# SyncE's order in the attention stage of a four-layer graph network: the turned pair's store and loads side by side

## The chip, the cores and the metric

The kernel runs on one core of a Trainium2 chip. The metric is the device time of one execution in microseconds (us), the median over the runs.

## The reference, cut to what matters

Four graph layers run in sequence on x of 4096 x 128 with one adjacency matrix of 4096 x 4096, each with a residual and a layer norm. The change lies in the third, a transformer convolution with four heads of width 32.

```python
x = _layernorm(x + _L0_gnn_ref(x, adj, ...), axis=-1)   # adj @ x, then a GRU cell
x = _layernorm(x + _L1_gnn_ref(x, adj, ...), axis=-1)   # normalised adj @ (x @ W)
x = _layernorm(x + _L2_gnn_ref(x, adj, ...), axis=-1)   # the attention below
x = _layernorm(x + _L3_gnn_ref(x, adj, ...), axis=-1)   # hyperbolic layer, adj @ xt

attn = jnp.einsum('nhc,mhc->hnm', q, k) / np.float32(np.sqrt(C))
mask = adj == 0.0
neg = jnp.where(mask[None], -jnp.inf, attn)
...
out = jnp.einsum('hnm,mhc->hnc', alpha, v)
```

## The kernel before

**Stages.** Layers 0 and 1 and the last one multiply the whole adjacency matrix, in 8 chunks of 512 columns that pass through a ring of 1 MB slots (`adj_cols`). Between them lies the attention, from about 570 to 1600 us of the span.

**The attention's tiles.** It works through 8 chunks of 512 rows; a chunk has 4 row blocks of 128 rows, and a row block is done in 2 sets of 2048 columns each. So there are 64 sets (set 0 to 63, eight to a chunk). A set is 16 units of 128 columns; every unit has the four heads. Everything is unrolled, and each engine has an order written out by hand, in places k (one per unit, 128 to a chunk).

- PE (TensorE): `scores` (L635, matmuls L647) writes the scores of a block of 1024 columns for one head, 13 heads ahead of the units. `turn_unit` (L667, L674) turns the probabilities of a unit into PSUM; ACT (L920) or VectorE (L1226) copies them to SBUF. `attend` (L678, L696) multiplies them with the values, four units at a time, 7 to 10 places later.
- VectorE: `mask` (L1197, L1211) adds scores and mask bias and takes the minimum. It also turns units 14 and 15 of every set itself, in 32 x 32 blocks, in `turn_blocks` (L1228, L1236) at places 3 and 5 of the next set.
- GpSimd: `mask_bias` (L1470, L1476) makes a mask bias from a loaded piece of the adjacency matrix (128 x 1024). It also runs the long row chain of the chunk before (`post_steps`, L1483 to L1489), in fixed slots between the masks.
- SyncE issues the loads and stores of the stage, in the order of `attention_loads` (L433).

**The turned pair.** Blocks that VectorE turned still lie in the wrong order of 32-row blocks. The pair (units 14 and 15 of a set, `GROUPS = ((14, 15),)`) therefore goes to DRAM in one store of 512 KB (`store_group`, L411, issue L417) and comes back in four loads of 128 KB (`load_group`, L419, issue L429). The loads wait for the store (`group_out`) and for PE to have used units 0 to 7 of the same set, whose slots they take (`unit_used`, L427). PE waits for them (`group_landed`) before unit 14, at place 19 counted from the set's first unit.

**What else is in SyncE's order.** `load_mask` (L395, issue L399) waits until GpSimd has made the bias two masks before (`bias_ready`), since the two input buffers alternate; it runs 7 masks ahead. `load_queries` (L402, issue L407) loads the queries of the row block after the next one, four DMAs of 64 KB, in every odd set. `store_xt` (L458, L460), in sets 48 and 56, saves a result tile `mx_g` that GpSimd overwrites in the next chain; `store_x3` (L480, L482) does the same for x3 once per chunk; `load_residuals` (L468, L477) ends the chunk. An instruction of SyncE that waits holds everything behind it in the order.

For each set the order is: the first mask; then in the second half the store, the second mask, `store_xt`, queries, `store_x3`, and last the pair's four loads.

Of the kernel before, what the change touches and what calls it, by code (L numbers as in the profile page):

```python
# [117 lines left out]

def groups_until(g):

    return g // UPS * len(GROUPS) + sum(group[-1] < g % UPS for group in GROUPS)


def block_turns(g):
# [4 lines left out]
def group_of(k):  # L129

    return [group for group in GROUPS if k % UPS in group][0]


def in_group(k):

    return group_of(k).index(k % UPS)

# [46 lines left out]
def build_program(nc, adj_cols, adj, x_tiles, x_t, w_msg, b_msg, w_ih, w_hh, b_ih, b_hh, w_gcn, b_gcn,  # L184
# [7 lines left out]
    xt_dram = nc.dram_tensor("xt_dram", [len(SPILLED), P, CHUNK], F32)  # L192
    group_dram = nc.dram_tensor("group_dram", [2, P, 2 * CHUNK], F32)
    k4_dram = nc.dram_tensor("k4_dram", [CHUNKS, 4, H, C, CHUNK], F32)

    with ExitStack() as ctx:
# [70 lines left out]
        group_slots = arena[:, RING + 10 * CHUNK:RING + 12 * CHUNK]  # L267
        group_blocks = stat_s[:, TILES - 2 * TPC:TILES, :].rearrange("p t f -> p (t f)")
        spilled = stat_s[:, SPILLED[0] * TPC:(SPILLED[-1] + 1) * TPC, :].rearrange("p t f -> p (t f)")
        adj_in = (arena[:, RING + 4 * CHUNK:RING + 6 * CHUNK], spilled)  # L270
        maskbias = [half_[:, i * BLOCK:(i + 1) * BLOCK] for half_ in
# [9 lines left out]

        def slots_of(group):
            i = group[0] % TURNED - 6
            return group_slots[:, i * CHUNK:(i + len(group)) * CHUNK]

# [40 lines left out]
        bias_ready = sem("bias_ready")  # L326
        xt_out, xt_in_place = sem("xt_out"), sem("xt_in_place")
        scores_ready = sem("scores_ready")
# [5 lines left out]
        unit_used = sem("unit_used")  # L334
        blocks_turned = sem("blocks_turned")
        group_out = sem("group_out")
        group_landed = sem("group_landed")
        rows_pe, rows_act, rows_dve, rows_pool = [sem(f"rows_{e}") for e in ("pe", "act", "dve", "pool")]
# [28 lines left out]
        def _(sp):  # L367
            def load_ring(layer, c, first, slots=SLOTS):

                for s in range(slots):  # L370
                    turn = layer * CHUNKS + c
                    if layer == 0 and first:
                        sp.dma_start(stat_x[:, s * JPS:(s + 1) * JPS, :].rearrange("p t f -> p (t f)"),
                                     x_tiles[:, s * JPS * P:(s + 1) * JPS * P]).then_inc(x_in[s], 16)
                    if first and layer == 2 and s % 4 == 0:
                        turned_before = (CHUNKS * SPC - 2 + s // 4 + 1) * UPS
                        sp.wait_ge(unit_turned, pe_turns(turned_before))
                        sp.wait_ge(blocks_turned, block_turns(turned_before))
                    if not first:
                        sp.wait_ge(ring_multiplied, (turn - 1) * SLOTS + s + 1)  # L380
                        if layer == 0 or is_zero(c):
                            sp.wait_ge(ring_summed, (turn - 1) * SLOTS + s + 1)
                    sp.dma_start(ring[:, s, :, :].rearrange("p j i -> p (j i)"),
                                 adj_cols[bass.ds(c, 1), s, :, :].rearrange("c p n -> (c p) n")
                                 ).then_inc(ring_landed[s], 16)
# [24 lines left out]

            def store_group(g):  # L411

                i, n = groups_until(g), len(group_of(g))
                sp.wait_ge(blocks_turned, block_turns(g + n))
                if i >= 2:
                    sp.wait_ge(group_landed, 16 * (P // C) * (i - 1))
                sp.dma_start(group_dram[i % 2, :, 0:n * CHUNK], group_blocks[:, 0:n * CHUNK]).then_inc(group_out, 16)  # L417

            def load_group(g):  # L419

                i, n = groups_until(g), len(group_of(g))
                slots = slots_of(group_of(g))
                sp.wait_ge(group_out, 16 * (i + 1))
                if i < len(GROUPS):
                    sp.wait_ge(gcn_x2_out, 16 * CHUNKS)
                if g + n > TURNED:
                    sp.wait_ge(unit_used, g + n - TURNED)  # L427
                for j in range(P // C):
                    sp.dma_start(slots[j * C:(j + 1) * C, :].rearrange("k (q n) -> k q n", q=P // C),  # L429
                                 group_dram[i % 2, :, j * n * P:(j + 1) * n * P].rearrange("(q k) n -> k q n", q=P // C)  # L430
                                 ).then_inc(group_landed, 16)

            def attention_loads(c):  # L433
                for st in range(SPC):
                    for half_set in range(2):
                        groups = [group for group in GROUPS if group[0] // UPB == half_set]
                        ahead = c * COLS + 2 * st + half_set + MASK_AHEAD
                        if half_set == 1:
                            for group in groups:
                                store_group(c * UPC + st * UPS + group[0])  # L440
                        if ahead < CHUNKS * COLS:
                            load_mask(ahead // COLS, ahead % COLS, False)
                        if half_set == 0:
                            for group in groups:
                                store_group(c * UPC + st * UPS + group[0])
                        if half_set == 1 and st == 0 and c - 2 in SPILLED:
                            store_xt(c - 2)
                        if half_set == 1 and st % SETS == 1:
                            ahead = c * TPC + st // SETS + 2
                            if ahead < CHUNKS * TPC:  # L450
                                load_queries(ahead // TPC, ahead % TPC, False)
                        if half_set == 1 and st == 4 and c > 0:
                            store_x3(c - 1)
                        for group in groups:
                            load_group(c * UPC + st * UPS + group[0])
                load_residuals(c)
# [5 lines left out]
            def load_xt():  # L462
                sp.wait_ge(bias_ready, CHUNKS * COLS)
                for i in range(len(SPILLED)):
                    sp.wait_ge(xt_out, 16 * (i + 1))
                    sp.dma_start(spilled[:, i * CHUNK:(i + 1) * CHUNK], xt_dram[i, :, :]).then_inc(xt_in_place, 16)
# [57 lines left out]
        def _(pe):  # L524
# [153 lines left out]
            def attend(c, k, first):  # L678
# [4 lines left out]
                if is_block_turned(k):  # L683
                    pe.wait_ge(group_landed, 16 * (P // C) * (groups_until(c * UPC + k) + 1))
                elif k in BY_VECTOR:
                    pe.wait_ge(unit_copied_dve, c * len(BY_VECTOR) + BY_VECTOR.index(k) + 1)
                else:
                    pe.wait_ge(unit_copied_act, c * len(BY_SCALAR) + BY_SCALAR.index(k) + 1)
                for h in range(H):
                    to = bank[h * C:(h + 1) * C, 7, st * P:(st + 1) * P]  # L690
                    if is_block_turned(k):
                        to = to.rearrange("c (q r) -> c q r", q=P // C)
                        weights = group_tiles(slots_of(group_of(k)), len(group_of(k)))[:, in_group(k), h, :, :]
                    else:
# [332 lines left out]
        def _(dve):  # L1027
# [169 lines left out]
            def mask(c, m, h, first):  # L1197
# [3 lines left out]
                if h == 0:  # L1201
                    dve.wait_ge(bias_ready, c * COLS + m + 1)
                    if not (first and m < 4):
                        dve.wait_ge(unit_turned, pe_turns((c * COLS + m - 3) * UPB))
                        dve.wait_ge(blocks_turned, block_turns((c * COLS + m - 3) * UPB))
                if hi:
# [21 lines left out]
            def turn_blocks(c, k):  # L1228

                st, u = k // UPS, k % UPS  # L1230
                i = groups_until(c * UPC + k)
                dve.wait_ge(exp_ready, (c * SPC + st) * H + H)
                if i > 0:
                    dve.wait_ge(group_out, 16 * i)
                n = len(group_of(k))
                dve.transpose(group_tiles(group_blocks[:, 0:n * CHUNK], n)[:, in_group(k), :, :, :],  # L1236
                              cols[:, st % SETS, :, u * P:(u + 1) * P].rearrange("p h (j k) -> p h j k", j=P // C)
                              ).then_inc(blocks_turned, 1)

# [162 lines left out]
        def _(pool):  # L1402
# [76 lines left out]
            def post_steps(c, factor_at=31):  # L1479
# [96 lines left out]
                def factor():  # L1576
# [3 lines left out]
                    tt("fac", s1, s1, t1, ALU.mult)  # L1580
                    if isinstance(c, int) and c == CHUNKS - 2:
                        pool.wait_ge(group_out, 16 * CHUNKS * SPC * len(GROUPS))
                    to = tiles(mx_g) if c in SPILLED else stat_s[:, c * TPC:(c + 1) * TPC, :]
# [112 lines left out]
```

## Time and profile before

| | |
|---|---|
| median of 3 runs | 1848.42 us (1846.78 to 1848.55) |
| the profiled execution | 1854.71 us |
| its span, first to last instruction | 1852.9 us |
| busy share PE / VectorE / ScalarE / GpSimd | 95% / 67% / 52% / 48% |
| mean granted TensorE clock over the span | 0.978 |

A row of a wait names the instruction that waited, then what ended the wait. In a timeline a line gives the start, the length, engine, source line and operation, and in brackets the idle time before it. `SPq` is SyncE's queue, whose instructions are issues and take about 0.3 to 0.45 us each; "x4" merges four. The granted clock is TensorE's, 1.00 for 2.4 GHz.

### The profile page before, as it was taken

To read this page: it belongs to the slowest core of one execution; us is meant where nothing else is said; L and a number is where in the kernel's file an instruction comes from. 1 tells how busy PE (TensorE), PEld (TensorE's weight loads), DVE (VectorE), ACT (ScalarE), POOL (GpSimd) and SP (SyncE) were. 2 spreads that over 40 slices of the span, in tenths; PEclk is the share of its full clock that TensorE was granted. 3 is DMA by queue.
4 is the path that set the end of the run, shared out by engine and by line. 5 is a ranking of instruction groups with operands and counts; after the bars stand their busy time and mean duration, and the time that the engine had idled before them with its cause. 6 is when DMAs were issued, how large, how long until landed. Compare 5 with 4: busy or idle time off the path is not lost.

```text
span 1852.9 us, 40409 instructions
## 1 busy us (share of the span) xinstructions
PE 1764.6 (95%) x14992; PEld 1163.3 (63%) x14992; DVE 1249.3 (67%) x2454; ACT 959.6 (52%) x1456; POOL 897.4 (48%) x853
## 2 busy tenths in 40 slices
PE   7999999999996999999999999999999999799996
PEld 3444444444444888877878878878778787444442
DVE  4777775222216999998989989979989899201322
ACT  0110110100004989898989978978989899201101
POOL 0111110111126556778687687777786886340111
PEclk9999999999997999999999999999999999899998
DMA  9857666799987555445444555454454543797791
GB/s 374 306 215 264 248 235 240 273 376 379 393 299 244 154 160 162 146 136 162 148 148 144 155 155 149 138 149 143 139 166 148 150 153 105 281 373 283 276 333 65
DMA packets 138525, 396.92 MB, mean 214 GB/s; under 512 B 16240, under 2 KB 67184, under 8 KB 113776
## 3 DMA queue, kind: packets, MB, share of 16 engines
q1 hardware_dynamic: 115776, 353.42, 55.9%
q10 hardware_dynamic: 20016, 32.78, 4.9%
q0 software_dynamic: 2560, 8.39, 1.5%
q8 instruction: 111, 1.82, 0.4%
q14 instruction: 62, 0.51, 0.1%
HBM read 333.19 MB, written 61.34 MB: 213 GB/s over the span
## 4 chain that ended last, share of the span: by engine, by line
PE 73%; POOL 10%; DMA 6%; DVE 4%; issue 3%; SPq 2%; ACT 0%; POOLq 0%; ACTq 0%; DVEq 0%
PE bank L540 32%; PE bank L674 14%; PE bank L647 10%; PE bank L696 9%; POOL arena L1476 3%; POOL small L1483 3%; DMA arena<-group_dram 2%; POOL early L1476 2%; DVE arena L1211 2%; DMA arena<-adj_cols 2%; DMA q_dram<-arena 1%; PE bank L528 1%; SPq L429 1%; PE bank L561 1%; PE bank L562 1%
## 5 line engine op out<-in xcount | busy, mean ns | idle before, releaser
L908 ACT ACTIVATE arena<-arena,small 128x2048 f32<-128x2048 f32 x256 | 512.3, 2001 | 0.0
L674 PE MATMUL bank<-ident,arena 128*128 128x128 f32 x3584 | 477.6, 275 | 0.7 <-ACT arena L908 0.7
L674 PEld LDWEIGHTS bank<-ident,arena 128*128 128x128 f32 x3584 | 423.4, 142 | 66.5 <-issue 3.5
L540 PE MATMUL bank<-arena,stat_s 128*128 128x512 f32 x1008 | 444.7, 598 | 9.7 <-DMA arena<-adj_cols 6.3
L920 ACT ACTIVATE arena<-bank 128x512 f32<-128x512 f32 x624 | 351.1, 596 | 112.4 <-PE bank L674 109.3
L647 PE MATMUL bank<-k,parts 128*128 128x512 f32 x1024 | 375.6, 449 | 13.3 <-DVE small L1211 7.1
L540 PEld LDWEIGHTS bank<-arena,stat_s 128*128 128x128 f32 x1008 | 191.2, 192 | 238.4 <-issue 236.7
L696 PE MATMUL bank<-arena,stat_x 128*32 128x128 f32 x8192 | 280.9, 277 | 27.2 <-DMA arena<-group_dram 27.2
L696 PEld LDWEIGHTS bank<-arena,stat_x 128*32 128x32 f32 x8192 | 207.9, 110 | 85.9 <-issue 48.8
L540 PE MATMUL bank<-arena,stat_x 128*128 128x512 f32 x512 | 230.8, 602 | 10.8 <-DMA arena<-adj_cols 8.5
L1226 DVE COPY arena<-bank 128x512 f32<-128x512 f32 x272 | 181.9, 676 | 44.0 <-PE bank L674 43.9
L647 PEld LDWEIGHTS bank<-k,parts 128*128 128x128 f32 x1024 | 157.3, 193 | 70.8 <-issue 41.6
L1211 DVE CUSTOM_DVE_ANT_0 arena<-bank,early,small 128x1024 f32<-128x1024 f32 x128 | 160.2, 1274 | 24.6 <-issue 18.5
L540 PEld LDWEIGHTS bank<-arena,stat_x 128*128 128x128 f32 x512 | 96.4, 192 | 127.4 <-issue 127.0
L1211 DVE CUSTOM_DVE_ANT_0 arena<-bank,arena 128x1024 f32<-128x1024 f32 x128 | 155.2, 1218 | 12.9 <-PE bank L674 8.9
L1211 DVE CUSTOM_DVE_ANT_0 arena<-bank,arena,small 128x1024 f32<-128x1024 f32 x128 | 160.5, 1278 | 1.5 <-PE bank L647 0.5
L1211 DVE CUSTOM_DVE_ANT_0 arena<-bank,early 128x1024 f32<-128x1024 f32 x128 | 155.2, 1213 | 6.7 <-PE bank L647 4.1
L1422 POOL TENSOR_SCALAR small<-small 128x4 f32<-128x4 f32 x32 | 13.0, 407 | 262.0 <-DVE small L1038 262.0
L1476 POOL TENSOR_SCALAR early<-arena 128x1024 bf16<-128x1024 f32 x32 | 116.3, 3634 | 32.2 <-DVE small L1211 25.6
L1476 POOL TENSOR_SCALAR arena<-arena 128x1024 bf16<-128x1024 f32 x32 | 116.5, 3641 | 24.2 <-DVE small L1211 13.9
L1476 POOL TENSOR_SCALAR early<-stat_s 128x1024 bf16<-128x1024 f32 x32 | 116.1, 3628 | 22.7 <-DVE small L1211 19.1
L1476 POOL TENSOR_SCALAR arena<-stat_s 128x1024 bf16<-128x1024 f32 x32 | 116.8, 3649 | 10.5 <-DVE small L1211 4.4
(155 smaller groups left out, 1425.7 us busy)
## 6 DMA issues: line engine op xcount, KB each, us to landing
arena<-adj_cols SPq DMA_DIRECT2D x190, 1024.0 KB, 6.4
arena<-adj SPq DMA_DIRECT2D x64, 512.0 KB, 4.8
stat_s<-adj SPq DMA_DIRECT2D x64, 512.0 KB, 4.4
group_dram<-stat_s SPq DMA_DIRECT2D x64, 512.0 KB, 3.0
arena<-group_dram SPq DMA_DIRECT2D x256, 128.0 KB, 2.9
k_dram<-arena ACTq DMA_DIRECT2D x32, 256.0 KB, 6.9
q_dram<-arena ACTq DMA_DIRECT2D x32, 256.0 KB, 11.7
k<-k_dram POOLq DMA_DIRECT2D x32, 256.0 KB, 8.4
```

The source lines that it names most:

```text
L429: sp.dma_start(slots[j * C:(j + 1) * C, :].rearrange("k (q n) -> k q n", q=P // C), group_dram[i % 2, :, j * n * P:(j + 1) * n * P].rearra ...
L528: last = pe.transpose(bank[:, dst_bank, t * P:(t + 1) * P], src[:, t * P:(t + 1) * P], ident[:, :])
L540: mm_ = pe.matmul(bank[:, to, :], stat[:, jt, :], ring[:, s, j, :], start=(jt == 0), stop=(jt == TILES - 1))
L647: last = pe.matmul(bank[:, u + i, :], parts[:, t % 2, h * P:(h + 1) * P], k4[:, h, at_:at_ + CHUNK], start=True, stop=True)
L674: last = pe.transpose(bank[:, b_, h * P:(h + 1) * P], cols[:, st % SETS, h, u * P:(u + 1) * P], ident[:, :])
L696: last = pe.matmul(to, stat_x[:, k % UPT, h * C:(h + 1) * C], weights, start=(u == 0), stop=(u == UPS - 1))
L908: act.activation(cols[:, s_, h, :], cols[:, s_, h, :], ACT.Exp, bias=shift[:, t % 2, 1, i:i + 1], scale=-1.0, accum_out=blocksum[:, t % 2, ...
L920: act.activation(turned[k % TURNED], bank[:, TURN_BANKS.bank(("unit", k)), :], ACT.Copy).then_inc(unit_copied_act, 1)
L1211: dve.tensor_tensor_reduce(out=cols[:, s_, h, hi * BLOCK:(hi + 1) * BLOCK], in0=bank[:, 2 * (h % 2):2 * (h % 2) + 2, :].rearrange("p b n - ...
L1226: dve.tensor_copy(turned[k % TURNED], bank[:, TURN_BANKS.bank(("unit", k)), :]).then_inc(unit_copied_dve, 1)
L1476: pool.tensor_scalar(maskbias[m % 4], adj_in[m % 2], 0.0, MASKED, ALU.is_equal, ALU.mult).then_inc(bias_ready, 1)
L1483: step(c, name, pool.tensor_tensor(out_, a, b, op))
```

## The change

In each set SyncE now issues: the first mask, the pair's store, the pair's four loads, the second mask, `store_xt`, queries, `store_x3`. The waits inside `load_group` stay, so SyncE stands there until the store has landed and PE has freed the slots.

The semaphores `blocks_turned`, `group_out` and `group_landed` become lists with one entry per group, and are counted in sets. There is still one group. The DRAM buffer has one place per group instead of two in turn, so a store waits for the landing of the loads of the set before, not of two sets before. VectorE's `mask` no longer waits for its own `blocks_turned`; the reloading of the spilled tiles (`load_xt`) waits for all stores as well.

```diff
-    group_dram = nc.dram_tensor("group_dram", [2, P, 2 * CHUNK], F32)
+    group_dram = nc.dram_tensor("group_dram", [len(GROUPS), P, 2 * CHUNK], F32)
...
-        group_blocks = stat_s[:, TILES - 2 * TPC:TILES, :].rearrange("p t f -> p (t f)")
         spilled = stat_s[:, SPILLED[0] * TPC:(SPILLED[-1] + 1) * TPC, :].rearrange("p t f -> p (t f)")
-        adj_in = (arena[:, RING + 4 * CHUNK:RING + 6 * CHUNK], spilled)
+        adj_in = (arena[:, RING + 4 * CHUNK:RING + 6 * CHUNK], spilled[:, 0:2 * CHUNK])
+        tail = stat_s[:, TILES - 2 * TPC:TILES, :].rearrange("p t f -> p (t f)")
+        blocks = [tail if len(group) == 2 else spilled[:, 2 * CHUNK:3 * CHUNK] for group in GROUPS]
...
-            def store_group(g):
-
-                i, n = groups_until(g), len(group_of(g))
-                sp.wait_ge(blocks_turned, block_turns(g + n))
-                if i >= 2:
-                    sp.wait_ge(group_landed, 16 * (P // C) * (i - 1))
-                sp.dma_start(group_dram[i % 2, :, 0:n * CHUNK], group_blocks[:, 0:n * CHUNK]).then_inc(group_out, 16)
-
-            def load_group(g):
-
-                i, n = groups_until(g), len(group_of(g))
-                slots = slots_of(group_of(g))
-                sp.wait_ge(group_out, 16 * (i + 1))
-                if i < len(GROUPS):
+            def store_group(g, i):
+
+                n = len(GROUPS[i])
+                sp.wait_ge(blocks_turned[i], n * (g + 1))
+                if g > 0:
+                    sp.wait_ge(group_landed[i], 16 * (P // C) * g)
+                sp.dma_start(group_dram[i, :, 0:n * CHUNK], blocks[i]).then_inc(group_out[i], 16)
+
+            def load_group(g, i):
+
+                n, slots = len(GROUPS[i]), slots_of(i)
+                sp.wait_ge(group_out[i], 16 * (g + 1))
+                if g == 0:
                     sp.wait_ge(gcn_x2_out, 16 * CHUNKS)
-                if g + n > TURNED:
-                    sp.wait_ge(unit_used, g + n - TURNED)
+                if g * UPS + GROUPS[i][-1] >= TURNED:
+                    sp.wait_ge(unit_used, g * UPS + GROUPS[i][-1] - TURNED + 1)
                 for j in range(P // C):
                     sp.dma_start(slots[j * C:(j + 1) * C, :].rearrange("k (q n) -> k q n", q=P // C),
-                                 group_dram[i % 2, :, j * n * P:(j + 1) * n * P].rearrange("(q k) n -> k q n", q=P // C)
-                                 ).then_inc(group_landed, 16)
+                                 group_dram[i, :, j * n * P:(j + 1) * n * P].rearrange("(q k) n -> k q n", q=P // C)
+                                 ).then_inc(group_landed[i], 16)
+
+            def load_mask_ahead(c, n):
+                ahead = c * COLS + n + MASK_AHEAD
+                if ahead < CHUNKS * COLS:
+                    load_mask(ahead // COLS, ahead % COLS, False)
 
             def attention_loads(c):
                 for st in range(SPC):
-                    for half_set in range(2):
-                        groups = [group for group in GROUPS if group[0] // UPB == half_set]
-                        ahead = c * COLS + 2 * st + half_set + MASK_AHEAD
-                        if half_set == 1:
-                            for group in groups:
-                                store_group(c * UPC + st * UPS + group[0])
-                        if ahead < CHUNKS * COLS:
-                            load_mask(ahead // COLS, ahead % COLS, False)
-                        if half_set == 0:
-                            for group in groups:
-                                store_group(c * UPC + st * UPS + group[0])
-                        if half_set == 1 and st == 0 and c - 2 in SPILLED:
-                            store_xt(c - 2)
-                        if half_set == 1 and st % SETS == 1:
-                            ahead = c * TPC + st // SETS + 2
-                            if ahead < CHUNKS * TPC:
-                                load_queries(ahead // TPC, ahead % TPC, False)
-                        if half_set == 1 and st == 4 and c > 0:
-                            store_x3(c - 1)
-                        for group in groups:
-                            load_group(c * UPC + st * UPS + group[0])
+                    g = c * SPC + st
+                    load_mask_ahead(c, 2 * st + 0)
+                    store_group(g, 0)
+                    load_group(g, 0)
+                    load_mask_ahead(c, 2 * st + 1)
+                    if st == 0 and c - 2 in SPILLED:
+                        store_xt(c - 2)
+                    if st % SETS == 1:
+                        ahead = c * TPC + st // SETS + 2
+                        if ahead < CHUNKS * TPC:
+                            load_queries(ahead // TPC, ahead % TPC, False)
+                    if st == 4 and c > 0:
+                        store_x3(c - 1)
                 load_residuals(c)
...
                 sp.wait_ge(bias_ready, CHUNKS * COLS)
+                for i in range(len(GROUPS)):
+                    sp.wait_ge(group_out[i], 16 * CHUNKS * SPC)
...
                 if is_block_turned(k):
-                    pe.wait_ge(group_landed, 16 * (P // C) * (groups_until(c * UPC + k) + 1))
+                    i = group_of(k)
+                    pe.wait_ge(group_landed[i], 16 * (P // C) * ((c * UPC + k) // UPS + 1))
...
-                        dve.wait_ge(blocks_turned, block_turns((c * COLS + m - 3) * UPB))
...
-                i = groups_until(c * UPC + k)
+                i = group_of(k)
                 dve.wait_ge(exp_ready, (c * SPC + st) * H + H)
-                if i > 0:
-                    dve.wait_ge(group_out, 16 * i)
-                n = len(group_of(k))
-                dve.transpose(group_tiles(group_blocks[:, 0:n * CHUNK], n)[:, in_group(k), :, :, :],
+                if c * SPC + st > 0:
+                    dve.wait_ge(group_out[i], 16 * (c * SPC + st))
```

## Rows read from the trace of the kernel before

**Rows 1.** The page's first part: busy time of each engine over the span.

```profile
PE 1764.6 (95%) x14992; PEld 1163.3 (63%) x14992; DVE 1249.3 (67%) x2454; ACT 959.6 (52%) x1456; POOL 897.4 (48%) x853
```

**Rows 2.** Waits of PE, 595 to 1600 us: total us, times, longest us.

```profile
PE bank L696 <- DMA arena<-group_dram: 27.2, 13, 3.5
PE bank L528 <- DVE arena L1047: 5.3, 7, 0.8
```

**Rows 3.** Timeline of PE in two stretches: start us, us, then the group.

```profile
842.56 0.65 PE L696 MATMUL bank<-arena,stat_x 128*32 128x128 f32 x16 [2.97 <-DMA arena<-group_dram]
...
1595.48 1.08 PE L696 MATMUL bank<-arena,stat_x 128*32 128x128 f32 x16 [3.35 <-DMA arena<-group_dram]
```

**Rows 4.** Waits of SyncE's own queue, whole span: total us, times, longest us.

```profile
SPq L427 <- PE bank L696: 152.3, 52, 6.3
```

**Rows 5.** Timeline of SyncE's queue, 811 to 837 us (sets 14 and 15).

```profile
811.87 0.34 SPq L417 DMA_DIRECT2D group_dram<-stat_s  x1
818.31 0.33 SPq L399 DMA_DIRECT2D arena<-adj  x1
818.74 3.11 SPq L429 DMA_DIRECT2D arena<-group_dram  x4
...
828.95 0.34 SPq L417 DMA_DIRECT2D group_dram<-stat_s  x1
834.07 0.33 SPq L399 DMA_DIRECT2D arena<-adj  x1
834.44 1.85 SPq L407 DMA_DIRECT2D parts<-q_dram  x4
836.39 1.80 SPq L429 DMA_DIRECT2D arena<-group_dram  x4
```

**Rows 6.** Windows around two PE waits: us, PE busy (matmuls), granted clock, DMA share, GB/s.

```profile
840.00:850.00 10.00, 7.44 (x78) 0.83 0.69 211
...
1220.00:1230.00 10.00, 6.50 (x52) 0.66 0.56 167
```

**Rows 7.** Timeline of SyncE's queue in an ordinary odd set (set 9).

```profile
735.41 0.34 SPq L417 DMA_DIRECT2D group_dram<-stat_s  x1
735.79 0.43 SPq L399 DMA_DIRECT2D arena<-adj  x1
736.26 2.26 SPq L407 DMA_DIRECT2D parts<-q_dram  x4
740.54 1.74 SPq L429 DMA_DIRECT2D arena<-group_dram  x4
```

**Rows 8.** Timeline of PE in the same set: the first scores of the next row block.

```profile
748.62 0.71 PE L647 MATMUL bank<-k,parts 128*128 128x512 f32 x2
```

**Rows 9.** DMA issues by tile: KB each, median us from issue to landing.

```profile
arena<-adj SPq DMA_DIRECT2D x64, 512.0 KB, 4.8
parts<-q_dram SPq DMA_DIRECT2D x128, 64.0 KB, 3.8
```

**Rows 10.** Source line L407, the query loads: spread of the landing times.

```profile
DMA to landing us min/median/max: 1.9/3.8/5.5
```

**Rows 11.** Timelines of GpSimd and VectorE: the mask of set 9's second half.

```profile
744.06 3.63 POOL L1476 TENSOR_SCALAR early<-arena 128x1024 bf16<-128x1024 f32 x1
...
766.14 1.21 DVE L1211 CUSTOM_DVE_ANT_0 arena<-bank,early 128x1024 f32<-128x1024 f32 x1
```

**Rows 12.** Timelines of SyncE, GpSimd and VectorE, set 48 and after: the spilled tile.

```profile
1357.51 0.79 SPq L460 DMA_DIRECT2D xt_dram<-arena  x1
1362.81 2.45 SPq L429 DMA_DIRECT2D arena<-group_dram  x4
...
1364.76 1.28 POOL L1483 TENSOR_TENSOR arena<-arena,wbr 128x512 f32<-128x512 f32 x1
...
1385.96 1.29 POOL L1483 TENSOR_TENSOR arena<-arena 128x512 f32<-128x512 f32 x1
...
1390.40 0.87 DVE L1031 BATCH_NORM_STATS2 small<-arena 128x6 f32<-128x128 f32 x4
```

More of the change, by code:

```diff
@@ L116, in pe_turns @@
     return g // UPC * len(PE_UNITS) + sum(k < g % UPC for k in PE_UNITS)
-def groups_until(g):
-    return g // UPS * len(GROUPS) + sum(group[-1] < g % UPS for group in GROUPS)
 def block_turns(g):
@@ L129, in group_of @@
 def group_of(k):
-    return [group for group in GROUPS if k % UPS in group][0]
+    return [i for i, group in enumerate(GROUPS) if k % UPS in group][0]
 def in_group(k):
-    return group_of(k).index(k % UPS)
+    return GROUPS[group_of(k)].index(k % UPS)
 class TurnBanks:
@@ L280, in group_tiles, with slots_of @@
             return ap.rearrange("p (b u h n) -> p u h b n", b=P // C, u=n, h=H)
-        def slots_of(group):
-            i = group[0] % TURNED - 6
-            return group_slots[:, i * CHUNK:(i + len(group)) * CHUNK]
+        def slots_of(i):
+            first, n = GROUPS[i][0] % TURNED - 6, len(GROUPS[i])
+            return group_slots[:, first * CHUNK:(first + n) * CHUNK]
         def tiles(ap):
@@ L326, in build_program @@
         bias_ready = sem("bias_ready")
-        xt_out, xt_in_place = sem("xt_out"), sem("xt_in_place")
         scores_ready = sem("scores_ready")
@@ L334, in build_program @@
         unit_used = sem("unit_used")
-        blocks_turned = sem("blocks_turned")
-        group_out = sem("group_out")
-        group_landed = sem("group_landed")
+        blocks_turned = [sem(f"blocks_turned{i}") for i in range(len(GROUPS))]
+        group_out = [sem(f"group_out{i}") for i in range(len(GROUPS))]
+        group_landed = [sem(f"group_landed{i}") for i in range(len(GROUPS))]
+        xt_out, xt_in_place = sem("xt_out"), sem("xt_in_place")
         rows_pe, rows_act, rows_dve, rows_pool = [sem(f"rows_{e}") for e in ("pe", "act", "dve", "pool")]
@@ L375, in load_ring @@
                     if first and layer == 2 and s % 4 == 0:
-                        turned_before = (CHUNKS * SPC - 2 + s // 4 + 1) * UPS
-                        sp.wait_ge(unit_turned, pe_turns(turned_before))
-                        sp.wait_ge(blocks_turned, block_turns(turned_before))
+                        sets = CHUNKS * SPC - 2 + s // 4 + 1
+                        sp.wait_ge(unit_turned, pe_turns(sets * UPS))
+                        for i, group in enumerate(GROUPS):
+                            sp.wait_ge(blocks_turned[i], sets * len(group))
                     if not first:
@@ L692, in attend @@
                         to = to.rearrange("c (q r) -> c q r", q=P // C)
-                        weights = group_tiles(slots_of(group_of(k)), len(group_of(k)))[:, in_group(k), h, :, :]
+                        weights = group_tiles(slots_of(i), len(GROUPS[i]))[:, in_group(k), h, :, :]
                     else:
@@ L1230, in turn_blocks @@
                 st, u = k // UPS, k % UPS
-                i = groups_until(c * UPC + k)
+                i = group_of(k)
                 dve.wait_ge(exp_ready, (c * SPC + st) * H + H)
-                if i > 0:
-                    dve.wait_ge(group_out, 16 * i)
-                n = len(group_of(k))
-                dve.transpose(group_tiles(group_blocks[:, 0:n * CHUNK], n)[:, in_group(k), :, :, :],
+                if c * SPC + st > 0:
+                    dve.wait_ge(group_out[i], 16 * (c * SPC + st))
+                dve.transpose(group_tiles(blocks[i], len(GROUPS[i]))[:, in_group(k), :, :, :],
                               cols[:, st % SETS, :, u * P:(u + 1) * P].rearrange("p h (j k) -> p h j k", j=P // C)
-                              ).then_inc(blocks_turned, 1)
+                              ).then_inc(blocks_turned[i], 1)
             def below_max(c, t):
@@ L1580, in factor @@
                     tt("fac", s1, s1, t1, ALU.mult)
-                    if isinstance(c, int) and c == CHUNKS - 2:
-                        pool.wait_ge(group_out, 16 * CHUNKS * SPC * len(GROUPS))
+                    if c == CHUNKS - 2:
+                        for i in range(len(GROUPS)):
+                            pool.wait_ge(group_out[i], 16 * CHUNKS * SPC)
                     to = tiles(mx_g) if c in SPILLED else stat_s[:, c * TPC:(c + 1) * TPC, :]
```

## The prediction

> **What bounds the kernel now.** I began with the busy times [rows 1]: PE, TensorE's matmuls, is busy 95% of the span and no other engine over 67%. The reader is to see that a microsecond counts only if PE loses it. The second view, PE's waits in the attention stage, lists little: 27.2 us in 13 waits for `arena<-group_dram`, and 5.3 us in seven small ones for VectorE [rows 2]. PE runs its 64 sets there almost without a gap, so the loads of the turned pair are what can be won.
>
> The timeline of PE gives the places [rows 3]. The thirteenth wait, 3.35 us at 1595.48, closes the last set, where no mask or query load is left and PE has no other work; the change doesn't touch what it waits for. The other twelve sum to 27.2 - 3.35 = 23.8 us, and lie in the last two sets of each of chunks 1 to 6.
>
> SyncE's queue says why [rows 4, 5]. Of 64 pair loads, 52 start when PE frees the slots (L427); twelve start later. In set 14 the store goes out at 811.87, the next instruction is a mask load that waits for GpSimd until 818.31, and the pair's loads follow it at 818.74. In set 15 the store is at 828.95, the mask at 834.07, four query loads take 1.85 us, and the pair starts at 836.39. Here GpSimd is behind with the row chain of the chunk before, and its mask delays loads that have nothing to do with masks.
>
> The granted clock adds to the price [rows 6]. PE's windows show 0.83 after the 2.97 us wait at 842.56 and 0.66 after the longest. Four windows of 10 us show 0.83 (1.7 us lost at most in each, since in part of it the clock is at 1.2 instead of 2.4 GHz) and one 0.66 (3.4 us): 10.2 us together.
>
> **The change, part by part.** *The pair's store and loads are put together, ahead of the set's second mask.* The twelve late loads then start at the later of the store's landing and PE's release. PE's release comes, as in an ordinary set, some 5.1 us after the store (735.41 to 740.54 [rows 7]): in set 14 at about 817.0 instead of 818.74, in set 15 at about 834 or earlier instead of 836.39. This removes 23.8 us of waits and, if the clock then stays up, up to 10.2 us. I take 10 of these, with 0 and 10.2 as bounds. In the second of each two sets the store itself can land late, beside the set's first mask; I keep 1 us in all for six such sets (bounds 0 and 6, up to 1 us each).
>
> *Mask loads go later.* In an ordinary set the second mask was issued 0.4 us after the store, at 735.79; now it follows the pair's loads, at 740.54 + 1.74 = 742.3, some 6.5 us later [rows 7]. It lands 4.8 us later [rows 9], at 747.1, and GpSimd, which started on it at 744.06, is delayed by 3 us; but VectorE reads the result first at 766.14 [rows 11]: 18 us of cover. In the sets where GpSimd is late its own backlog sets the mask's time, and nothing changes. Cost 0; without that cover it would be up to 3 us a set.
>
> *Query loads go later, and here the cover is thin.* In every odd set, 30 times, four query loads used to start at 736.26; now they come after the pair and the mask. From the start of the pair's loads L: 1.74 us for these, 0.43 and a gap for the mask, three more issues of 0.47, so the last query DMA starts at L + 3.7 and lands 3.8 us later by the median [rows 9]: L + 7.5, and L + 7.7 where the bytes queue a little. PE reads them for the first scores of the next row block at 748.62, L + 8.1 [rows 8]. The margin was over 6 us; it becomes some 0.4 us. Landing times run from 1.9 to 5.5 us [rows 10], and four pair loads take 3.11 us instead of 1.74 in some sets [rows 5], so about half of these sets would come late, by some 0.5 to 1.5 us. What is queued behind: PE's scores, then everything. I put the mean over all 30 at 0.4 us, 12 us in sum (estimate). Bounds: 0 if all lands in time; with every query 1 us later than by these medians, mean about 0.9, 27 us.
>
> By the Trainium skill (DMA: Bandwidth & Descriptors, Anatomy of one DMA) a DMA takes about 2.0 us fixed plus its bytes over 436 GB/s, a fit of the GpSimd path. For 64 KB that is 2.15 us, the last query DMA would land at about L + 5.9, no set would wait, and the sum would be 31 us of gain instead of 19. The trace has 3.8 us here, and I go by the trace.
>
> *Stores of `xt` and `x3` go later.* In sets 48 and 56 the spilled tile's store moves from 1357.51 to behind the pair and the mask, about 1365, and lands near 1370 instead of 1362; GpSimd overwrites the tile at 1364.76, so it waits some 5 us. Its row chain ends at 1385.96 + 1.29 and VectorE reads it at 1390.40: 3.2 us of cover [rows 12]. Two times 2 us are left on VectorE, half of which I let reach PE: 2 us (bounds 0 and 4). The `x3` store has half a chunk of time; cost 0.
>
> *Semaphores per group, one DRAM buffer instead of two, a VectorE wait dropped.* There is one group, so the counts name the same events. The store now waits for the previous set's loads, which PE has multiplied with before that store is due. VectorE's dropped wait was for its own long finished work. At 0, bounds -1 and +1.
>
> Sum: 23.8 + 10 - 1 - 12 - 2 = 19 us (18.8). The profiled execution took 1854.7 us (span 1852.9), so it would be 1836; the median of the runs, 1848.4, is 6.3 below it, and 1848.4 - 18.8 gives 1829.5.
>
> **The rivals.** *A. The likeliest: the waits go, late queries take a third back.* 1829.5, own range 1821 to 1839.
>
> *B. The queries are in time.* For it: by the medians they land 0.4 us early. 33.8 - 3 leaves 30.8 us of gain: 1817.6. Against: the spread in rows 10 and the slow issues in rows 5.
>
> *C. The queries come over 1 us late in most odd sets.* The pair's four loads move 512 KB in small pieces, the mask another 512 KB, and the queries stand behind both. 30 waits of 0.9 us give back 27 of the 30.8 and leave 1844.6. It decides against the change from about 1.2 us over the medians, where 30 waits of 1.03 us equal the 30.8 won; at 1.5 us over (30 waits of 1.3) the kernel takes 1848.4 - 30.8 + 39 = 1856.6. For it: the landing spread in rows 10. Against: before the change the queries stood behind a store and a mask of the same size. The Trainium skill (same page, Queues, rings and completion order) says that each DMA engine takes the descriptors of one issuing engine's queue in ring order; by that rule the queries are served last, which is this case.
>
> *D. It doesn't do what it says.* If the late loads were held by L427 or by the store's landing, PE's waits would remain: within 3 us of before. Rows 5 speak against it, since both had come before 818.31 and 834.07.
>
> **How the numbers follow.** A 0.55, B 0.2, C 0.22, D 0.03. A change under 0.2%, 3.7 us, is about what a measurement of this kernel can't tell from none. Of C, 0.12 end faster, 0.04 within that bound and 0.06 slower. Faster: 0.55 + 0.2 + 0.12 = 0.87; same: 0.04 + 0.03 of D = 0.07; slower: 0.06. Range: from 1815, the full 33.8 us, to 1844, the cheap end of C.
>
> **What would show it.** Right: PE's waits for `arena<-group_dram` fall to about 3.4 us in one or two, and the granted clock is 1.00 from 600 to 1590. SyncE's queue shows the pair's loads about 5 us after the store in every set. A new row, PE L647 waiting for `parts<-q_dram`, sums to about 12 us in 10 to 20 waits. GpSimd waits once or twice some 5 us in chunks 6 and 7 before its L1483. Wrong: if that new row stays under 3 us (B), or passes 25 us or pulls the clock down (C), or if the old row stays (D).

## The result, and the profile after

The changed kernel takes 1843.05 us (median of 13 runs, 1836.95 to 1848.52), the kernel before 1848.56 us (13 runs, 1846.3 to 1855.68). The ratio is 0.9965, 95% interval 0.9952 to 0.9979: faster, by 5.5 us between the medians, 3.9 to 8.9 us by the interval. The forecast was 1829.5, a gain of 18.8 us. The measured time lies inside the range of 1815 to 1844 us, but outside case A's own range of 1821 to 1839. The traced executions took 1854.71 us before and 1848.52 us after, the slowest of the changed kernel's 13, so their figures run above those of a median execution.

The waits of PE in the attention stage, 595 to 1600 us, come first again (total us, times, longest us). They answer to [rows 2].

```profile
PE bank L642 <- DMA parts<-q_dram: 15.4, 16, 3.0
PE bank L523 <- DVE arena L1043: 5.3, 7, 0.8
PE bank L535 <- DMA arena<-adj_cols: 5.2, 1, 5.2
PE bank L642 <- DVE small L1206: 4.2, 7, 1.7
PE bank L692 <- DMA arena<-group_dram: 3.7, 1, 3.7
PE bank L669 <- ACT arena L904: 0.7, 1, 0.7
PE bank L669 <- DVE arena L1250: 0.5, 1, 0.5
```

The line that was 27.2 us in 13 waits [rows 2] is down to the one wait that closes the last set. In its place stands `parts<-q_dram`, 15.4 us in 16 waits, and L642 also waits 4.2 us for VectorE. (The wait for `adj_cols` belongs to the next stage, which starts earlier now and so falls in the window.)

SyncE's queue in set 9 shows the new order. It answers to [rows 7].

```profile
739.52 0.33 SPq L414 DMA_DIRECT2D group_dram<-stat_s  x1
744.65 1.76 SPq L425 DMA_DIRECT2D arena<-group_dram  x4
746.45 0.43 SPq L396 DMA_DIRECT2D arena<-adj  x1
746.92 2.74 SPq L404 DMA_DIRECT2D parts<-q_dram  x4
```

In sets 14 and 15, where the mask once held the pair's loads, store and loads now stand as in any set. This answers to [rows 5]: the pair's loads start 5.3 and 4.5 us after the store, where they started 6.9 and 7.4 us after it.
```profile
816.85 0.34 SPq L414 DMA_DIRECT2D group_dram<-stat_s  x1
822.20 1.75 SPq L425 DMA_DIRECT2D arena<-group_dram  x4
823.99 0.43 SPq L396 DMA_DIRECT2D arena<-adj  x1
832.42 0.35 SPq L396 DMA_DIRECT2D stat_s<-adj  x1
833.49 0.33 SPq L414 DMA_DIRECT2D group_dram<-stat_s  x1
838.02 1.75 SPq L425 DMA_DIRECT2D arena<-group_dram  x4
```

SyncE's own waits over the whole span, to be read beside [rows 4], say the same of all sets: each of the 64 pair loads now starts when PE frees the slots (L423), where 52 did.

```profile
SPq L423 <- PE bank L692: 322.2, 64, 9.3
```

PE's timeline for the scores behind the queries, which answers to [rows 8]: set 9 waits 0.33 us, and set 47 has the longest wait of all.

```profile
753.62 0.73 PE L642 MATMUL bank<-k,parts 128*128 128x512 f32 x2 [0.33 <-DMA parts<-q_dram]
```

```profile
1345.86 0.73 PE L642 MATMUL bank<-k,parts 128*128 128x512 f32 x2 [2.95 <-DMA parts<-q_dram]
1381.70 0.66 PE L669 MATMUL bank<-ident,arena 128*128 128x128 f32 x4 [0.45 <-DVE arena L1250]
```

Around that wait of 2.95 us lies the only window between 600 and 1580 us with a lower granted clock, 0.83; those that showed 0.83 and 0.66 in [rows 6] are at 1.00 (columns: us, PE, PEld, DVE, ACT, POOL busy with counts, clock, DMA share, GB/s).

```profile
1340.00:1350.00 10.00, 7.05 (x86) 5.75 (x88) 5.26 (x10) 6.09 (x10) 9.14 (x7) 0.83 0.71 206
...
840.00:850.00 10.00, 9.50 (x124) 7.59 (x113) 8.51 (x16) 7.92 (x13) 8.39 (x10) 1.00 0.87 246
1220.00:1230.00 10.00, 9.09 (x124) 7.46 (x128) 6.86 (x14) 8.00 (x11) 9.14 (x7) 1.00 0.39 132
```

The source line of the query loads, L404, against [rows 10]: the landing time has a longer tail, and 19 weight loads wait 20.0 us (PEld stands in front of the matmul, so part of its waiting is covered).

```profile
L404 SPq DMA_DIRECT2D parts<-q_dram x128: 343/432/1312, 541.0 to 1531.6; - x128
...
  PEld bank L642: 20.0, 19
  PE bank L642: 15.4, 16
...
DMA to landing us min/median/max: 2.2/4.1/7.3
```

The spilled tile after set 48, on SyncE, GpSimd, VectorE, to be read beside [rows 12]: GpSimd waits 7.22 us for the store to land, and VectorE, whose cover was 3.2 us, waits 3.06 us for the end of GpSimd's chain.

```profile
1357.12 0.43 SPq L396 DMA_DIRECT2D arena<-adj  x1
1357.60 0.43 SPq L453 DMA_DIRECT2D xt_dram<-arena  x1
...
1363.32 1.28 POOL L1477 TENSOR_TENSOR arena<-arena,wbr 128x512 f32<-128x512 f32 x1 [7.22 <-DMA xt_dram<-arena]
...
1385.85 0.88 DVE L1027 BATCH_NORM_STATS2 small<-arena 128x6 f32<-128x128 f32 x4 [3.06 <-POOL arena L1477]
```

### The profile page after: what moved, and what is told of

Its sections match the earlier page's. It is cut to its first block and busy times, and to the rows that moved or that the text cites. A ratio compares the mean times of both kernels' runs of the same rounds, so it can differ in the third digit from the quotient of the medians.

```text
span 1846.7 us, 40348 instructions
## 1 busy us (share of the span) xinstructions
PE 1759.7 (95%) x14992; PEld 1158.7 (63%) x14992; DVE 1255.3 (68%) x2454; ACT 959.8 (52%) x1456; POOL 898.4 (49%) x853
## 5 line engine op out<-in xcount | busy, mean ns | idle before, releaser
L642 PE MATMUL bank<-k,parts 128*128 128x512 f32 x1024 | 371.2, 444 | 35.1 <-DMA parts<-q_dram 15.4
L692 PE MATMUL bank<-arena,stat_x 128*32 128x128 f32 x8192 | 278.0, 276 | 3.8 <-DMA arena<-group_dram 3.7
L692 PEld LDWEIGHTS bank<-arena,stat_x 128*32 128x32 f32 x8192 | 208.6, 110 | 59.6 <-issue 48.0
L642 PEld LDWEIGHTS bank<-k,parts 128*128 128x128 f32 x1024 | 154.8, 190 | 97.5 <-issue 40.3
L1206 DVE CUSTOM_DVE_ANT_0 arena<-bank,arena 128x1024 f32<-128x1024 f32 x128 | 155.4, 1220 | 18.1 <-PE bank L669 14.3
```

Source lines behind the costliest of these rows:

```text
L642: last = pe.matmul(bank[:, u + i, :], parts[:, t % 2, h * P:(h + 1) * P], k4[:, h, at_:at_ + CHUNK], start=True, stop=True)
L692: last = pe.matmul(to, stat_x[:, k % UPT, h * C:(h + 1) * C], weights, start=(u == 0), stop=(u == UPS - 1))
L1206: dve.tensor_tensor_reduce(out=cols[:, s_, h, hi * BLOCK:(hi + 1) * BLOCK], in0=bank[:, 2 * (h % 2):2 * (h % 2) + 2, :].rearrange("p b n - ...
```

## The experiments

Each run starts from the changed kernel and reorders what `attention_loads` issues in a set. Written short: M1 and M2 the masks, S the pair's store, L its four loads, X the store of `xt`, Q the queries, X3 the store of `x3`. The changed kernel is M1 S L M2 X Q X3, the kernel before M1 S M2 X Q X3 L. All arithmetic is the reference's in every run. Four kernels first, on one chip.

**Queries first, `xt` still late: M1 S Q L M2 X X3.**

```diff
                     store_group(g, 0)
-                    load_group(g, 0)
-                    load_mask_ahead(c, 2 * st + 1)
-                    if st == 0 and c - 2 in SPILLED:
-                        store_xt(c - 2)
                     if st % SETS == 1:
...
                             load_queries(ahead // TPC, ahead % TPC, False)
+                    load_group(g, 0)
+                    load_mask_ahead(c, 2 * st + 1)
+                    if st == 0 and c - 2 in SPILLED:
+                        store_xt(c - 2)
```

> The four query loads go between the pair's store and its loads; the second mask stays behind the loads, as in the changed kernel. Theory 1 (the queries are late because their bytes stand in SyncE's queue behind the pair's loads and the mask): PE's waits for parts<-q_dram fall from 15.4 us to under 1 us, and the time falls by 20 to 24 us against the changed kernel, to about 1821 us. Theory 2 (PE loses through the late masks: GpSimd waits 110 us for them in the trace of the changed kernel, and its row chain holds VectorE): the query waits go, but VectorE's waits for GpSimd remain and take their place, and the time stays above 1836 us.

Measured: 1825.89 us, ratio to before 0.9881 (0.9859 to 0.9902), 17.2 us under the changed kernel. PE waits for no query and no window from 600 to 1560 us shows a lower clock. The late queries cost about 17 us by the medians and 15.5 us by the two ratios (0.9965 and 0.9881), not 12. That is less than the 20 to 24 us expected for this run; L642's waits for VectorE went up from 4.2 to 5.8 us.

The traces can be compared by the first and last start of L692, the multiplications with the values, in the changed kernel and then in this run:

```profile
L692 PE MATMUL bank<-arena,stat_x x8192: 272/273/423, 601.9 to 1591.1; 128*32 128x128 f32 x200
...
L692 PE MATMUL bank<-arena,stat_x x8192: 272/273/298, 600.1 to 1569.1; 128*32 128x128 f32 x200
```

So the attention stage is 20.2 us shorter in this trace (989.2 and 969.0 us). The spans differ by 24.5 us; the other 4.3 us lie outside the stage, where the two kernels do the same, and are most likely a difference between two executions.

**`xt` and `x3` stores early, queries still late: M1 S X X3 L M2 Q.**

```diff
                     store_group(g, 0)
-                    load_group(g, 0)
-                    load_mask_ahead(c, 2 * st + 1)
                     if st == 0 and c - 2 in SPILLED:
                         store_xt(c - 2)
+                    if st == 4 and c > 0:
+                        store_x3(c - 1)
+                    load_group(g, 0)
+                    load_mask_ahead(c, 2 * st + 1)
```

> The stores of xt and x3 go between the pair's store and its loads; mask and queries stay behind the loads. Theory 1: GpSimd's 11.7 us of waiting for xt_dram goes, VectorE's BATCH_NORM_STATS waits in chunks 6 and 7 and PE's two waits of 1.6 to 1.7 us for VectorE go, 4 to 5 us gained: about 1838 us. Theory 2 (the masks are what delays the row chain): those VectorE waits stay at 2 to 3 us and the time is within 2 us of the changed kernel's 1843.

Measured: 1839.57 us, ratio 0.9946 (0.9926 to 0.9967), 3.5 us under the changed kernel. The interval overlaps that of the changed kernel (0.9952 to 0.9979), so the times alone don't show this gain; the waits do. PE's waits in the attention stage of this run:

```profile
PE bank L642 <- DMA parts<-q_dram: 13.2, 18, 2.2
...
PE bank L642 <- DVE small L1206: 1.3, 5, 0.5
```

The query waits stay; L642's wait for VectorE falls from 4.2 to 1.3 us. That wait was the spilled tile's, by way of GpSimd and VectorE.

**Both first: M1 S X Q X3 L M2.** Only L and M2 have changed places with the rest.

```diff
                     store_group(g, 0)
-                    load_group(g, 0)
-                    load_mask_ahead(c, 2 * st + 1)
...
                         store_x3(c - 1)
+                    load_group(g, 0)
+                    load_mask_ahead(c, 2 * st + 1)
```

> Queries and the stores of xt and x3 go between the pair's store and its loads; only the second mask stays behind the loads. Theory 1: what is left is the late masks alone, at no more than 2 us in sum, so nearly all of the 35.6 us that PE lost in sets 13 to 15 of each chunk is won: 1814 to 1817 us, with the granted clock at 1.00 through the stage. Theory 2: above 1830 us.

Measured: 1822.85 us, ratio 0.9864 (0.9845 to 0.9883), 25.7 us under before. Both theories missed: one had 1814 to 1817 us, the other above 1830. Its SyncE queue in set 9: the queries fill the time in which the pair's loads wait anyway for the store and for PE, and L stands 5.1 us behind S as before.

```profile
735.50 0.33 SPq L414 DMA_DIRECT2D group_dram<-stat_s  x1
735.87 2.26 SPq L404 DMA_DIRECT2D parts<-q_dram  x4
740.64 1.73 SPq L425 DMA_DIRECT2D arena<-group_dram  x4
742.41 0.43 SPq L396 DMA_DIRECT2D arena<-adj  x1
```

PE's waits in the stage show what is late next, VectorE and ScalarE, 5.1 us in 14 waits:

```profile
PE bank L669 <- DVE arena L1250: 1.9, 6, 0.5
PE bank L642 <- ACT arena L916: 1.8, 4, 0.5
PE bank L642 <- DVE small L1206: 1.4, 4, 0.4
```

**The old order with the new semaphores and buffers: M1 S M2 X Q X3 L.**

```diff
                     store_group(g, 0)
-                    load_group(g, 0)
                     load_mask_ahead(c, 2 * st + 1)
...
                         store_x3(c - 1)
+                    load_group(g, 0)
```

> SyncE's old order (mask, store, mask, xt, queries, x3, loads) with the new semaphores, the single DRAM buffer and the VectorE wait dropped. Theory 1 and 2 (the order is all): within 2 us of before, and PE's 27 us of waits for arena<-group_dram in 13 places. Theory 3 (semaphores or the single buffer have a cost or a gain of their own that hid part of the order's gain): 3 us or more away from before.

Measured: 1847.28 us, ratio 1.0007 (0.9989 to 1.0025). PE waits 26.3 us in 11 waits for `arena<-group_dram`, and its windows at 840, 950 and 1220 us show a clock of 0.83 again. Order is what counts; semaphores, DRAM buffer and the dropped wait together change the time by something between -2.0 and +4.6 us, which isn't told from nothing.

Two more asked what it is that makes the queries late, and whether the late masks cost anything.

**Queries behind the pair but ahead of the mask: M1 S L Q M2 X X3.**

```diff
                     load_group(g, 0)
-                    load_mask_ahead(c, 2 * st + 1)
-                    if st == 0 and c - 2 in SPILLED:
-                        store_xt(c - 2)
                     if st % SETS == 1:
...
                             load_queries(ahead // TPC, ahead % TPC, False)
+                    load_mask_ahead(c, 2 * st + 1)
+                    if st == 0 and c - 2 in SPILLED:
+                        store_xt(c - 2)
```

> The changed kernel with one swap: the query loads go before the second mask instead of after it, still behind the pair's loads. They are issued 0.48 us earlier, and 512 KB fewer stand ahead of them. Theory A (it is the bytes ahead in SyncE's queue): the last query lands 1.5 to 2 us earlier counted from the start of the pair's loads, PE's waits for parts<-q_dram fall from 15.4 us to under 3 us, and the time is 12 to 18 us under the changed kernel's: 1825 to 1831 us. Theory B (it is only the later issue): the landing moves by 0.5 us, the waits fall to about 9 us and the time to about 1836 us.

Measured: 1832.6 us, ratio 0.9915 (0.9902 to 0.9928), on another chip than the four kernels above, where the kernel before takes 1847.81 us. PE never waits for a query, as theory A has it; the time is 1.6 us above its range. SyncE's queue in set 9:

```profile
740.44 1.75 SPq L425 DMA_DIRECT2D arena<-group_dram  x4
742.24 2.91 SPq L404 DMA_DIRECT2D parts<-q_dram  x4
745.19 0.44 SPq L396 DMA_DIRECT2D arena<-adj  x1
```

The last query lands at 747.1, L + 6.7; in the changed kernel it lands at 753.6, L + 8.9. Over all 30 sets the traces have a median of L + 5.9 here and of L + 8.8 (7.5 to 10.4) in the changed kernel. Of these 2.9 us, 0.5 us is the later issue of the fourth query (L + 3.2 and L + 3.7). The rest is its time from issue to landing, 2.35 and 4.7 us by the median, and goes with the mask's 512 KB ahead of the queries. The pair's 512 KB ahead of them do nothing of the kind: here, behind the pair alone, all query loads have a median of 2.5 us, and in the run with the queries first 2.6 us. The time is 6.3 us above that of the run with the queries first by the ratios. I can place only part of it: L642's waits for VectorE are 14 instead of 9, and one wait of 0.44 us for the pair is back.

**The new order only in sets 6 and 7 of chunks 1 to 7, with X, Q and X3 ahead of the pair everywhere.** The other sets keep M2 ahead of the pair.

```diff
+                    if c > 0 and st >= 6:
...
+                        load_group(g, 0)
+                        load_mask_ahead(c, 2 * st + 1)
+                    else:
+                        load_mask_ahead(c, 2 * st + 1)
...
+                        load_group(g, 0)
```

> In the last two sets of chunks 1 to 7 SyncE's order is store, xt, queries, x3, the pair's loads, second mask; in all other sets the old order with the second mask right behind the store. Theory: the 7 us that the kernel with queries and stores first still loses against a set without waits (0.4 us in the second and the last set of each chunk) come from the later masks, through GpSimd's row chain and VectorE. Then these go too, GpSimd's waits for arena<-adj fall from 97 us to under 5 us, and the time is 1815 to 1819 us. Rival: they come from the missing stalls, since GpSimd is now the one that is behind; then they stay, and the time is 1821 to 1824 us.

Measured: 1826.5 us, ratio 0.9886 (0.9872 to 0.9901), on the same chip as the run before: not faster than with all masks behind the pair, and above the ranges of both theories. GpSimd's long waits for masks are gone from it, and PE's small waits for VectorE and ScalarE are as large as in the run with both first. In return PE waits 6.5 us in five waits for the pair. One of them closes the last set as in every run; the other four, 3.4 us, stand in the first sets of chunks 3, 4, 6 and 7, where the mask is ahead of the pair. So late masks cost nothing that these runs show. That masks ahead of the pair cost a little in other sets too is shown by the waits and not by the time, whose interval overlaps that of the run with both first.

Last, on one chip, a test of what holds PE in the order with both first, beside that order once more.

**Both first, and VectorE's `norm_h` 4 places later.** It is a short reduction at the end of each chunk that has to wait for GpSimd's squares (6.4 us in six waits), with VectorE's unit copies and masks queued behind it. ScalarE's logarithm, which follows it, moves along.

```diff
-            def post_steps(c, norm_h_at=113):
+            def post_steps(c, norm_h_at=117):
...
-                post = post_steps(c - 1, 107 if last_chunk else 113) if not first else {}
+                post = post_steps(c - 1, 107 if last_chunk else 117) if not first else {}
...
-                                                   115 if last_chunk else 119)
+                                                   115 if last_chunk else 123)
```

> Stores, queries and x3 ahead of the pair, both masks behind it (the order of the run 'both first', 1822.85 us), and in addition VectorE's reduction of GpSimd's squares (norm_h) taken 4 places later in chunks 2 to 6, with ScalarE's logarithm behind it also 4 places later. Theory: what is left of the loss at the ends of the chunks comes from this reduction, for which VectorE waits 6.4 us in six waits there, so that its masks, copies and transposes are late for PE afterwards (PE's waits for L1250, L916 and L1206 together 5.1 us in 14). Then L1297's wait falls under 2 us, these waits of PE under 3 us, and the time is 1819 to 1821.5. Rival: VectorE and ScalarE are late by their own work alone (the row chain of the chunk before beside the unit copies); L1297's wait falls all the same, PE's waits stay near 5 us and the time stays within 1822 to 1825.

Measured: 1819.87 us, ratio 0.9832 (0.9812 to 0.9852). PE's waits for the three lines in the stage:

```profile
PE bank L669 <- DVE arena L1250: 0.5, 1, 0.5
PE bank L642 <- DVE small L1206: 0.2, 1, 0.2
PE bank L669 <- ACT arena L916: 0.2, 1, 0.2
```

VectorE no longer waits at `norm_h`, and the 5.1 us have become 0.9. The mechanism is shown by the trace; the time, 3.5 us under the neighbour below, agrees in size, though the two intervals overlap.

**Both first, once more.**

> The order of the run 'both first' once more, unchanged, as the neighbour of the run with the later reduction on the same chip. Both theories: 1822 to 1825, PE's waits for L1250, L916 and L1206 together about 5 us, none for the queries, the clock never at its lower level in the attention stage.

Measured: 1823.39 us, ratio 0.9848 (0.983 to 0.9866). PE's three lines sum to 4.6 us in 12 waits. Queries never hold PE.

## Why the prediction was right in its mechanism and wrong in its size

Case A, "the waits go, late queries take a third back", is the case that the trace shows, but two steps of its sum failed, and the gain was 5.5 us instead of 18.8. The larger one is the step from the removed waits and the clock to the time: 23.8 + 10 - 1 = 32.8 us were entered in full, and what PE would wait for next was put at nothing without a reason. The runs show 25.7 us in its place (21.6 to 28.7 by the interval), 7.1 us less (points 1, 2 and 7). The other is the query term: 12 us forecast, about 17 measured, some 5 us more (point 3). The stores add 1.5 us (point 4). The parts of the sum were the right ones but for the one left out. That the time came within 2 us of the 1844.6 of rival C is luck: C has 27 us for queries on top of the full gross gain, and neither was there.

1. *The twelve late pair loads.* Right. 27.2 us in 13 waits [rows 2] became 3.7 us in one. The 1 us kept for stores landing late isn't seen as a wait of PE for the pair.
2. *The clock.* Right but for one window. I took 10 us; the five windows with a lower clock are gone, and a late query brought a new one (0.83 at 1340 to 1350), worth 1.7 us at most by the way I priced [rows 6].
3. *Queries.* The second term that failed: 30 sets at 0.4 us, 12 us. The measured price is 17.2 us (changed kernel against queries first) and, from the other pair of orders, 16.7 us (1839.57 against 1822.85); by the ratios it is 15.5 and 15.2 us. Two parts of it were off. First, landing: I had L + 7.7, "where the bytes queue a little", from a median of 3.8 us that was measured with the queries ahead of the pair's loads [rows 7, 9]. Behind pair and mask the median of the 30 sets is L + 8.8. The fourth query was issued at L + 3.7, as reckoned, but took 4.7 us to land. The fifth experiment shows what does it: with the mask behind the queries, and the pair still ahead, the median is L + 5.9 and no set waits. Second, a wait of PE is not its whole price. In the traces the stage is 20.2 us longer with late queries, while the 16 waits sum to 15.4 us and the clock's part is 1.7 us at most. Most of the other 3 us lies in the same sets, each of which is some 0.3 us longer than PE's wait in it; why is open. (This is the slowest of the changed kernel's executions, so the 15.4 us aren't to be set against the 17.2 us of the medians.) Rival C named the bytes ahead of the queries as the cause, and put it at 0.9 us a wait; the mean is 17 / 30 = 0.57 us a set, between A and C. Its prices don't follow from the margin either: a query 1 us over the medians, at L + 8.7, is 0.6 us late against L + 8.1, not 0.9.
4. *Stores of `xt`.* Mechanism right, size too small. Forecast 2 us with a bound of 4; measured 3.5 us (changed kernel against stores first) and 3.0 us (1825.89 against 1822.85), each with overlapping intervals. I let half of VectorE's lateness reach PE. The trace says nearly all of it: VectorE waits 3.06 us (the lines after set 48 above), and L642's two long waits for VectorE in the changed kernel, 1.66 and 1.57 us, are gone with the stores first.
5. *Masks later.* Right at 0. The sixth experiment took GpSimd's waiting for masks away, 97 us in the run with both first, and gained nothing.
6. *Semaphores, buffer, dropped wait.* Right at 0 within the noise: ratio 1.0007 (0.9989 to 1.0025).
7. *What the sum left out.* After the stall it never asked which engine is late next. With queries and stores out of the way, PE waits 5.1 us in 14 short waits for VectorE and ScalarE, and most of that is one early reduction that stands at a wait for GpSimd. These 5.1 us are most of the 7.1 us missing from the gross gain (4 to 11 by the interval); the rest isn't told from noise. With the old order (the fourth run) PE shows 0.2 us of such waits in the stage, which fits that the long ones had covered them.

The runs can be put in a row: before 1848.56, minus 25.7 for the pair's new place gives 1822.85 (both first); plus 16.7 for late queries 1839.57; plus 3.5 for the late `xt` store 1843.05. That is a chain of differences and closes by construction; what supports it is that the other order of the two steps gives 3.0 and 17.2. My gross gain was 32.8 us. The run with `norm_h` later has 31 us by its ratio (27 to 35), so the gross figure agrees with the runs once nothing else is in the way. (A later `norm_h` with the old order was not run; its PE waits there, 0.2 us, leave little to gain.)

The Trainium skill (DMA: Bandwidth & Descriptors, Anatomy of one DMA) has about 2.0 us plus bytes over bandwidth for one DMA, a fit of the GpSimd path; that makes 2.15 us for 64 KB (estimate). With the queries ahead of the pair the trace agrees nearly: their median from issue to landing is 2.6 us, and behind the pair alone it is 2.5 us. Behind pair and mask it is 4.1 us, up to 7.3, for which the fit has no term. The rule of the Trainium skill (same page, Queues, rings and completion order) that each DMA engine takes the descriptors of one issuing engine's queue in ring order fits the changed kernel and the fifth experiment, in which no query issued ahead of the mask came late.

## What to carry to other kernels

When a load is moved behind others in one queue, take its landing time from what will stand ahead of it, not from a median measured in its old place, and put it against when it is needed; here the margin was 0.4 us by the median and minus 0.7 us by the landings (L + 8.8 against L + 8.1). Not every load ahead counts alike: a 512 KB mask right ahead did harm, four pair loads of the same size in sum did not. A queue whose next instruction must wait for another engine has free time in front of that wait: short, urgent loads belong there (between store and pair loads the queries cost nothing that a trace shows), long ones with cover belong behind. And once the large wait on the bounding engine is priced, look for the engine that was late behind it.

## What the runs showed of the hardware that I had not expected

A mask load of 512 KB with a single issue of 0.43 us, moved from ahead of the four queries to behind them, brings the last query 2.2 us earlier in set 9 (L + 8.9 to L + 6.7) and 2.9 us by the median of 30 sets. The pair's loads ahead of the queries leave the median from issue to landing at 2.5 us; with pair and mask ahead it is 4.1 us, and with store and mask ahead, in the kernel before, 3.8 us.

A wait of PE of 2.95 us stands in a window with a granted clock of 0.83, that is, part of it at 1.2 instead of 2.4 GHz; the 15 shorter waits for queries in the same run, up to 1.57 us, left the clock at 1.00. In the run with the stores first the clock fell after a wait of 1.84 us at 877.87 (0.92 from 870 to 880), but not after one of 2.17 us at 722.34. In the kernel before it fell after 2.37 us at 953.09 and not after 2.60 us at 1463.18. So the length of the last wait alone does not tell in these traces whether the clock falls. Where it fell, the price was above the wait: set 47 took 19.2 us in the changed kernel and 15.0 us with both first, 4.2 us for a wait of 2.95 us (a set is taken here from the start of its first multiplication with the values to that of the next set). With the shorter waits a set was some 0.3 us longer than its wait.
